# Pauses between all scattered row transfers, and routing one iteration earlier, in a fused attention and mixture-of-experts kernel

## The chip, the cores and the metric

The kernel runs on one NeuronCore of one Trainium2 chip. Its time is the device time of one execution in microseconds (us). The engines are TensorE (PE in the rows), VectorE (DVE), ScalarE (ACT), GpSimd (POOL) and SyncE (SP). SP and ACT also start DMA transfers; the rows name their queues SPq and ACTq.

## The reference, cut to what matters

16 batches of 100 rows of 256 features. Each batch attends over its own context with 16 heads; the result is added to the rows; each row is then normalised, 8 of 32 experts are chosen for it, and their weighted outputs and the output of two shared experts are added.

```python
x = x + xattn(layernorm(x), ctx)            # softmax over causal scores, 16 heads
h = layernorm(x)
scores = sigmoid(h @ gate_w.T)
sc = scores + gate_bias                      # 8 groups of 4 experts; the best 4 groups stay
tki = top_k(masked(sc), 8)[1]                # 8 experts for each row
tkw = 2.5 * scores[tki] / sum(scores[tki])
routed = sum over the 8 experts of tkw * (silu(h @ w_gate) * (h @ w_up)) @ w_down
shared = silu(h @ sh_gate.T) * (h @ sh_up.T) @ sh_down.T
out = x + routed + shared
```

## The kernel before, in words

The program is written out by hand, one stream of instructions for each engine, with semaphores between them. It has four stages.

**Projections** (to about 47 us): keys, values and queries of all 16 batches.

**Attention**, a loop `for i in range(NB)` on each engine, one batch in each iteration. DVE's iteration is `maximum(i)` (L592), `differences(i)` (L601), `residual(i - 2)` (L610 to L618), `shift(i - 2)` (L622) and `outputs_scaled(i - 1)` (L627, L629). ACT takes the exponentials (L428), copies the turned probabilities (L434), finishes the second norm (L439) and takes the tanh of the router's logits (L451). PE computes scores (L872, L877), turns the probabilities (L898), multiplies them with the values (`values`, L924 and L931, which raises `pv_psum`), projects (L941), turns the normed rows (L951) and computes the logits (L884). POOL has one instruction in the chain of the second norm, the power in `row_numbers(B)` (L359), for which DVE's `shift(B)` waits (`rstd2_ready`).

**Routing and scattering**, woven into the attention. Batches are routed in pairs p = 0 to 7. `route(p)` (L646 to L673) chooses the experts on DVE; `positions(p)` (L910 to L913), inside `values` on PE, counts the rows ahead of each row; `positions_read(p)` (L681) and `destinations(p)` (L687 to L693) on DVE turn this into eight row numbers for each row, and raise `dest_ready`. POOL then issues for each batch eight indirect DMAs (`rows_to_experts`, L364), each of which writes the 100 rows of the batch (1,156 bytes each) to places in the DRAM tensor `slots`, where the rows of an expert lie together. For the first 10 batches a memset of a scratch tile `pause` (L370) stands behind each of these DMAs. POOL runs `row_numbers(B)` and `rows_to_experts(B - 5)` in turn, and the last five batches behind the loop.

**Behind the attention**: `shared_gate_up`, `shared_gate` and so on work out part of the shared experts on PE, ACT and DVE; the counts (`count_psum`, L741) and the table of 132 tiles (L747 to L752) follow from the last pair's destinations. 32 DMAs `slots<-pad` fill the end of each expert's rows, 16 issued by SP (L292) once `pad_ready` is raised, and 16 by ACT (L493), which stand behind ACT's fourth shared tanh (L475). SP then waits for all scattered rows, for all pads and for the table, and starts the loads of the tiles (L304). **The tiles**: 132 tiles of 128 rows go through their experts, and POOL adds each result into DRAM with one indirect DMA (L389). At the end three sums are loaded, added and written out.

DVE executes in program order, so all behind a `wait_ge` in its stream waits too; the same holds for each other engine.

Of the kernel before, what the change touches and what calls it, by code (L numbers as in the profile page):

```python
# [18 lines left out]
NB = 16  # L19
# [14 lines left out]
TOPK = 8  # L34
# [27 lines left out]
def block_kernel(nc, x, ctx_t, w_attn, w_gate_t, col_bias, row_bias, gate_bias, w_exp, consts, out_t):  # L62
# [3 lines left out]
    with ExitStack() as top:  # L66
# [88 lines left out]
        pause = tmp("pause", [S, 176])  # L155
# [167 lines left out]
        def _(pool):  # L323
# [37 lines left out]
            def rows_to_experts(B):  # L361
                pool.wait_ge(dest_ready, B // 2 + 1)
                for r in range(TOPK):
                    pool.indirect_dma_start(slots[:], bass.IndirectOffsetOnAxis(ap=dest[:, B % XR, r:r + 1], axis=0),  # L364
                                            xr[:, B % XR, :], None).then_inc(rows_out[B % XR], 16)
                    if B < 10:

                        if B or r:
                            pool.wait_ge(paused, TOPK * B + r)
                        pool.memset(pause[:], 0.0).then_inc(paused, 1)  # L370

            pool.wait_ge(xt_lo_ready, NG)
            pool.wait_ge(v_psum, 2 * NG)
            pool.wait_ge(q_psum, KC * NG)
            for B in range(NB):
                row_numbers(B)
                if B >= 5:
                    rows_to_experts(B - 5)
            for B in range(NB - 5, NB):
                rows_to_experts(B)  # L380

            pool.wait_ge(zero_out, 16 * (2 * NSUM - 1))
# [152 lines left out]
        def _(v):  # L535
# [69 lines left out]
            def residual(B):  # L605
                v.wait_ge(xb_ready, B // BG + 1)
                v.wait_ge(proj_psum, B + 1)
                if B >= 2:
                    v.wait_ge(ht_ready, B - 1)
                v.tensor_tensor(x_all[:, B, :], ps[0:S, 7, 0:D], x_all[:, B, :], ALU.add).then_inc(x1_ready, 1)  # L610
                v.wait_ge(x1_ready, B + 1)
                v.bn_stats(st2[:], x_all[:, B, :]).then_inc(st2_done, 1)
                v.wait_ge(st2_done, B + 1)
                if B >= 4:
                    v.wait_ge(h1_ready, B - 3)
                v.bn_aggr(mv2[:, B % 4, :], st2[:]).then_inc(mv2_done, 1)
                v.wait_ge(mv2_done, B + 1)
                v.tensor_scalar(ve2[:, B % 4:B % 4 + 1], mv2[:, B % 4, 1:2], EPS, None, ALU.add).then_inc(var2_ready, 1)  # L618

            def shift(B):  # L620
                v.wait_ge(rstd2_ready, B + 1)
                v.scalar_tensor_tensor(nmr2[:, B % 4:B % 4 + 1], mv2[:, B % 4, 0:1], -1.0, rstd2[:, B % 4:B % 4 + 1], ALU.mult,  # L622
                                       ALU.mult).then_inc(shift_ready, 1)
# [71 lines left out]
            for i in range(NB):  # L695
                maximum(i)
                differences(i)
                if i >= 2:
                    residual(i - 2)
                if i >= 6 and i % 2 == 0:  # L700
                    route(i // 2 - 3)
                if i >= 2:
                    shift(i - 2)
                if i >= 1:
                    v.wait_ge(pv_psum, i)
                    if i >= 7 and i % 2 == 1:
                        positions_read((i - 7) // 2)
                    outputs_scaled(i - 1)
                if i >= 7 and i % 2 == 1:
                    destinations((i - 7) // 2)  # L710

            def shared_gate(n):
                s = n % 2
# [7 lines left out]
                v.tensor_copy(y_sh[:, :, group_cols(c)], ps[:, 2:2 + KC, 0:TG]).then_inc(sy_ready, 1)  # L721

            residual(14)
            outputs_scaled(15)
            shift(14)
            route(5)
            residual(15)
            shift(15)
            shared_gate(0)
            positions_read(5)  # L730
            destinations(5)
            route(6)
            shared_gate(1)
            positions_read(6)
# [81 lines left out]
        def _(t):  # L816
# [98 lines left out]
            def values(B):  # L915

                t.wait_ge(pt_ready, RG * (B + 1))
                if B:
                    t.wait_ge(ot_ready, B)
                for m in range(KC):  # L920
                    for p in range(2):
                        for r in range(RG):
                            h = 8 * m + 2 * r + p
                            t.matmul(ps[32 * r:32 * r + 32, 6, m * S:(m + 1) * S], v_g[B // BG][:, B % BG, 32 * h:32 * h + 32],  # L924
                                     pt[:, r, (2 * m + p) * S:(2 * m + p + 1) * S], start=(p == 0), stop=(p == 1),
                                     skip_group_check=True)
                if B >= 6 and B % 2 == 0:
                    positions(B // 2 - 3).then_inc(pos_psum, 1)
                for p in range(2):
                    for r in range(RG):  # L930
                        last = t.matmul(ps[32 * r:32 * r + 32, 6, KC * S:2 * KC * S], ones_pad[:, p, :],  # L931
                                        pt[:, r, :].rearrange("k (m p q) -> k m p q", m=KC, p=2)[:, :, p, :],
                                        start=(p == 0), stop=(p == 1), skip_group_check=True)
                last.then_inc(pv_psum, 1)
# [70 lines left out]
            shared_gate_up(0)  # L1005
            t.wait_ge(tanh_ready, 13)
            logits(13, 4, TG)
            t.wait_ge(ot_ready, NB)
            positions(5).then_inc(pos_psum, 1)
            turn_rows(14)  # L1010
            shared_gate_up(1)
            logits(14, 7, D + KC * S)
# [165 lines left out]
```

## Time and profile before

| | |
|---|---|
| median of 3 runs | 616.83 us (616.48 to 617.9) |
| the profiled execution, its own time | 620.36 us |
| its span, first to last instruction | 618.4 us |
| its mean granted TensorE clock | 0.857 |
| first scattered transfer on POOL | 117.02 us |
| start of the last scattered transfer | 314.25 us |
| start of the first tile load | 333.45 us |
| start of the first and of the last add | 344.10 and 587.92 us |

All stretches are in us from the start of the span of the one profiled execution. A wait written in brackets at the end of a row is the idle time of that engine just before the row, with the engine and line that ended it; "remote" and "another core or an unknown queue" there mean that the profile found no event that ended it at that moment, and "issue" that the engine waited for nothing that the profile shows.

### The profile page before, as it was taken

The numbers are of one execution on the slowest core, as the hardware profiler recorded it, in microseconds if no ns is written. First come the engines' busy times: TensorE is split into PE (matmuls) and PEld (weight loads), VectorE is DVE, ScalarE is ACT, GpSimd is POOL, SyncE is SP. The second block draws the span as 40 slices with busy tenths as digits, with TensorE's granted clock in tenths as the row PEclk, the third lists the DMA queues.
The fourth block names the chain that finished last, engine by engine and source line by source line (L and its number), as shares of the span: only waits on it lengthen the run. The fifth ranks groups of instructions, "written<-read, shape, count | busy, mean of one in ns | idle before, by whom it ended". The sixth has DMA issues, their size and how long they took to land.

```text
span 618.4 us, 11702 instructions
## 1 busy us (share of the span) xinstructions
PE 463.4 (75%) x3088; PEld 349.2 (56%) x3089; DVE 344.1 (56%) x1022; ACT 208.9 (34%) x610; POOL 391.7 (63%) x404
## 2 busy tenths in 40 slices
PE   2997986986788474632033999999899999999964
PEld 2895664754455352310012877787787787777633
DVE  5974789777576834621011555555555555555347
ACT  3443465323234320100000554444444444444300
POOL 7560000487877878677730688888888888888810
PEclk9996899579778757666555999999999999999995
DMA  7239130172236227234467577788788778884065
GB/s 210 79 133 351 48 128 29 30 231 87 76 81 223 79 64 271 76 90 119 121 206 180 102 140 140 137 146 141 139 144 142 139 139 143 138 142 95 1 227 198
DMA packets 64792, 82.94 MB, mean 134 GB/s; under 512 B 14272, under 2 KB 53824, under 8 KB 64756
## 3 DMA queue, kind: packets, MB, share of 16 engines
q1 hardware_dynamic: 35252, 52.14, 27.4%
q0 software_dynamic: 27200, 27.98, 26.1%
q10 hardware_dynamic: 2304, 2.37, 1.4%
q8 instruction: 19, 0.31, 0.2%
q14 instruction: 17, 0.14, 0.1%
HBM read 42.67 MB, written 43.93 MB: 140 GB/s over the span
## 4 chain that ended last, share of the span: by engine, by line
PE 23%; issue 21%; POOL 17%; DMA 12%; DVE 12%; another core or an unknown queue 9%; ACTq 2%; ACT 2%; POOLq 1%; SPq 0%; DVEq 0%
POOL slots L364 9%; DMA sums<-ysb,tin 9%; PE ps L1059 7%; POOL sums L389 4%; PE ps L1073 3%; DVE rden L627 2%; PE ps L823 2%; POOL pause L370 2%; PE ps L1050 2%; ACTq L493 2%; DMA fin<-sums 2%; PE ps L988 1%; DVE prob L601 1%; PE ps L941 1%
## 5 line engine op out<-in xcount | busy, mean ns | idle before, releaser
L389 POOL DMA_INDIRECT sums<-ysb,tin x132 | 204.9, 1552 | 69.3 <-ACT ysb L512 33.0
L364 POOL DMA_INDIRECT slots<-xr,dest x128 | 127.8, 998 | 46.8 <-issue 28.7
L1059 PE MATMUL ps<-w_all,hts 128*128 x528 | 137.6, 383 | 8.2 <-issue 5.1
L1059 PEld LDWEIGHTS ps<-w_all,hts 128*128 128x128 f32 x528 | 99.7, 191 | 25.8 <-issue 12.6
L760 DVE COPY hts<-ps 128x256 f32<-128x256 f32 x132 | 56.0, 425 | 80.9 <-PE ps L1050 61.9
L512 ACT ACTIVATE ysb<-ps 128x256 f32<-128x256 f32 x132 | 50.6, 383 | 101.8 <-DMA sums<-ysb,tin 96.0
L1073 PE MATMUL ps<-w_all,ats 128*128 x264 | 83.4, 398 | 0.2 <-ACT ats L504 0.2
L1050 PE MATMUL ps<-cst,tin 128*128 128x128 f32 x264 | 51.6, 278 | 11.6 <-DMA tin<-slots 9.8
L769 DVE SCALAR_TENSOR_TENSOR act_t<-opened_t,tin,ps 128x128 f32<-128x128 f32 x132 | 45.9, 348 | 20.9 <-DVE opened_t L764 12.8
L498 ACT ACTIVATE opened_t<-ps 128x128 f32<-128x128 f32 x132 | 36.3, 275 | 53.7 <-PE ps L1059 44.8
L1050 PEld LDWEIGHTS ps<-cst,tin 128*128 128x128 f32 x264 | 36.6, 142 | 29.1 <-issue 16.7
L898 PE MATMUL ps<-cst,prob 100*100 100x100 f32 x256 | 38.3, 296 | 17.4 <-ACT prob L428 15.3
L359 POOL TENSOR_TENSOR rstd<-ve,cst 100x1 f32<-100x1 f32 x16 | 9.1, 570 | 62.2 <-DVE ve L618 62.2
L764 DVE SCALAR_TENSOR_TENSOR opened_t<-opened_t,ps 128x128 f32<-128x128 f32 x132 | 37.1, 281 | 18.8 <-issue 9.6
L898 PEld LDWEIGHTS ps<-cst,prob 100*100 100x100 f32 x256 | 28.4, 154 | 28.2 <-ACT prob L428 21.1
L941 PE MATMUL ps<-wo,ot 128*100 128x256 f32 x64 | 24.7, 525 | 22.7 <-DVE ot L629 22.7
L1073 PEld LDWEIGHTS ps<-w_all,ats 128*128 128x128 f32 x264 | 39.6, 189 | 3.5 <-issue 0.6
L504 ACT ACTIVATE ats<-ps 128x128 f32<-128x128 f32 x132 | 37.0, 280 | 10.0 <-PE ps L1067 6.8
L998 PE MATMUL ps<-sh_act,w_sh 128*128 128x400 f32 x32 | 15.2, 606 | 33.5 <-issue 28.7
L1067 PE MATMUL ps<-cst,act_t 128*128 128x128 f32 x132 | 37.4, 283 | 3.3 <-DVE act_t L769 2.3
L434 ACT ACTIVATE pt<-ps 100x400 f32<-100x400 f32 x64 | 31.2, 501 | 22.6 <-PE ps L898 18.1
L428 ACT ACTIVATE prob<-prob 100x400 f32<-100x400 f32 x64 | 33.1, 535 | 13.6 <-DVE prob L601 11.7
(156 smaller groups left out, 687.2 us busy)
## 6 DMA issues: line engine op xcount, KB each, us to landing
tin<-slots SPq DMA_DIRECT2D x132, 144.5 KB
w_all<-w_exp SPq DMA_DIRECT2D x3, 2304.0 KB
fin<-sums SPq DMA_DIRECT2D x12, 400.0 KB
sums<-pad SPq DMA_DIRECT2D x2, 1664.0 KB, 8.3
w_all<-w_exp SPq DMA_DIRECT2D x1, 2688.0 KB
slots<-pad SPq DMA_DIRECT2D x17, 144.5 KB, 2.3
slots<-pad ACTq DMA_DIRECT2D x16, 144.5 KB
sums<-ysb,tin POOLq DMA_INDIRECT x132
```

Source lines behind the costliest of these rows:

```text
L364: pool.indirect_dma_start(slots[:], bass.IndirectOffsetOnAxis(ap=dest[:, B % XR, r:r + 1], axis=0), xr[:, B % XR, :], None).then_inc(rows_ ...
L389: pool.indirect_dma_start(sums[j % NSUM][:], bass.IndirectOffsetOnAxis(ap=tin[:, j % RING, ID:ID + 1].bitcast(U32), axis=0), ysb[:, j % YR ...
L504: a.activation(ats[:, s % 2, :], ps[:, 4 + s % 2, 0:P], ACT.Copy).then_inc(at_ready, 1)
L512: a.activation(ysb[:, s % YR, :], ps[:, 6 + s % 2, 0:D], ACT.Copy).then_inc(yt_ready, 1)
L760: v.tensor_copy(hts[:, s % 2], ps[:, s % 2, 0:KC * P].rearrange("p (k t) -> p k t", k=KC)).then_inc(lt_ready, 1)
L764: v.scalar_tensor_tensor(opened_t[:, 2 + s % 2, :], opened_t[:, s % 2, :], 1.0, ps[:, 2 + s % 2, 0:FI], ALU.add, ALU.mult).then_inc(opened, 1)
L769: v.scalar_tensor_tensor(act_t[:, s % 2, :], opened_t[:, 2 + s % 2, :], tin[:, s, bass.ds(e + WT, 1)], ps[:, 2 + s % 2, FI:2 * FI], ALU.mu ...
L898: last = t.transpose(ps[0:S, 4 + r % 2, j * S:(j + 1) * S], prob[:, B % 2, r, j * S:(j + 1) * S], ident[0:S, 0:S])
L1050: last = t.transpose(ps[:, s % 2, k * P:(k + 1) * P], tin[:, s, k * P:(k + 1) * P], ident)
L1059: last = t.matmul(ps[:, 2 + s % 2, 0:2 * FI].rearrange("p (t n) -> p t n", t=2), hts[:, s % 2, k, :], w[:, k], start=(k == 0), stop=(k == ...
L1067: t.transpose(ps[:, 4 + s % 2, 0:P], act_t[:, s % 2, :], ident).then_inc(at_psum, 1)
L1073: t.matmul(ps[:, 6 + s % 2, 0:D], ats[:, s % 2, :], w_all[:, bass.ds(e, 1), 2 * D:].rearrange("p o n -> p (o n)"), start=True, stop=True). ...
```

## The change

Three things are edited. First, the memset of `pause` follows every scattered DMA, where it followed those of batches 0 to 9. Second, on DVE `route(p)` moves from iteration 2p + 6 to iteration 2p + 5, and `destinations(p)` from 2p + 7 to 2p + 6; both, and `outputs_scaled`, now stand ahead of `shift` in the iteration. PE's `positions(p)` moves from `values(2p + 6)` to `values(2p + 5)`. Third, POOL scatters batch B - 4 behind `row_numbers(B)`, where it scattered batch B - 5.

```diff
                     pool.indirect_dma_start(slots[:], bass.IndirectOffsetOnAxis(ap=dest[:, B % XR, r:r + 1], axis=0),
                                             xr[:, B % XR, :], None).then_inc(rows_out[B % XR], 16)
-                    if B < 10:
-
-                        if B or r:
-                            pool.wait_ge(paused, TOPK * B + r)
-                        pool.memset(pause[:], 0.0).then_inc(paused, 1)
+
+                    if B or r:
+                        pool.wait_ge(paused, TOPK * B + r)
+                    pool.memset(pause[:], 0.0).then_inc(paused, 1)
...
             for B in range(NB):
                 row_numbers(B)
-                if B >= 5:
-                    rows_to_experts(B - 5)
-            for B in range(NB - 5, NB):
+                if B >= 4:
+                    rows_to_experts(B - 4)
+            for B in range(NB - 4, NB):
                 rows_to_experts(B)
...
                 if i >= 2:
                     residual(i - 2)
+                if i >= 1:
+                    v.wait_ge(pv_psum, i)
+                    if i >= 6 and i % 2 == 0:
+                        positions_read(i // 2 - 3)
+                    outputs_scaled(i - 1)
                 if i >= 6 and i % 2 == 0:
-                    route(i // 2 - 3)
+                    destinations(i // 2 - 3)
+                if i >= 5 and i % 2 == 1:
+                    route((i - 5) // 2)
                 if i >= 2:
                     shift(i - 2)
-                if i >= 1:
-                    v.wait_ge(pv_psum, i)
-                    if i >= 7 and i % 2 == 1:
-                        positions_read((i - 7) // 2)
-                    outputs_scaled(i - 1)
-                if i >= 7 and i % 2 == 1:
-                    destinations((i - 7) // 2)
...
             residual(14)
+            v.wait_ge(pv_psum, NB)
+            positions_read(5)
             outputs_scaled(15)
+            destinations(5)
             shift(14)
-            route(5)
             residual(15)
             shift(15)
             shared_gate(0)
-            positions_read(5)
-            destinations(5)
             route(6)
...
-                if B >= 6 and B % 2 == 0:
-                    positions(B // 2 - 3).then_inc(pos_psum, 1)
+                if B >= 5 and B % 2 == 1:
+                    positions((B - 5) // 2).then_inc(pos_psum, 1)
...
             t.wait_ge(tanh_ready, 13)
             logits(13, 4, TG)
-            t.wait_ge(ot_ready, NB)
-            positions(5).then_inc(pos_psum, 1)
             turn_rows(14)
```

On DVE, the end of the iteration that gives pair 0 its destinations; before, this is iteration 7 (`ve` is the last row of `residual(5)`, `nmr` is the shift):

```order
L618 TENSOR_SCALAR ve<-mv 100x1 [waits mv2_done]
L622 SCALAR_TENSOR_TENSOR nmr<-mv,rstd 100x1 [waits rstd2_ready]
L681 TENSOR_TENSOR rt<-ps,ebase 100x64 [waits pos_psum,tables_ready,pv_psum]
L627 RECIPROCAL rden<-ps 128x200 [waits pv_psum]
L629 TENSOR_TENSOR ot<-ps,rden 128x200 [waits rden_ready]
L687 SCALAR_TENSOR_TENSOR rt<-rt 100x64 [waits pos_ready]
L688 MAX best_d<-rt 100x8 [waits routing_step]
L688 MAX best_d<-rt 100x8
L690 TENSOR_SCALAR dest<-best_d 100x16 [waits weights_ready,routing_step]
```

The same place in the change, which is now iteration 6 (`ve` is the last row of `residual(4)`; the lines are one lower here):

```order
L617 TENSOR_SCALAR ve<-mv 100x1 [waits mv2_done]
L680 TENSOR_TENSOR rt<-ps,ebase 100x64 [waits pos_psum,tables_ready,pv_psum]
L626 RECIPROCAL rden<-ps 128x200 [waits pv_psum]
L628 TENSOR_TENSOR ot<-ps,rden 128x200 [waits rden_ready]
L686 SCALAR_TENSOR_TENSOR rt<-rt 100x64 [waits pos_ready]
L687 MAX best_d<-rt 100x8 [waits routing_step]
L687 MAX best_d<-rt 100x8
L689 TENSOR_SCALAR dest<-best_d 100x16 [waits weights_ready,routing_step]
L691 TENSOR_TENSOR run_mid<-mask_m 100x32
L692 TENSOR_TENSOR run<-run,run_mid 100x32 [waits routing_step]
L621 SCALAR_TENSOR_TENSOR nmr<-mv,rstd 100x1 [waits rstd2_ready]
```

The shift, which waits for POOL, has moved from ahead of the destinations to behind them, and the wait for `pv_psum` from behind the shift to ahead of it.

On POOL, the end of the scattering before, from the last `row_numbers` on:

```order
L357 IOTA xr 100x1 [waits rows_out7]
L359 TENSOR_TENSOR rstd<-ve,cst 100x1 [waits var2_ready]
L364 DMA slots<-xr,dest 55424x289 [waits dest_ready]
L364 DMA slots<-xr,dest 55424x289 x7
L364 DMA slots<-xr,dest 55424x289 [waits dest_ready]
L364 DMA slots<-xr,dest 55424x289 x7
```

In the change the rows there are these, and they go on in pairs of a DMA and a memset to the end:

```order
L357 IOTA xr 100x1 [waits rows_out7]
L359 TENSOR_TENSOR rstd<-ve,cst 100x1 [waits var2_ready]
L364 DMA slots<-xr,dest 55424x289 [waits dest_ready]
L369 MEMSET pause 100x176 [waits paused]
L364 DMA slots<-xr,dest 55424x289
L369 MEMSET pause 100x176 [waits paused]
L364 DMA slots<-xr,dest 55424x289
L369 MEMSET pause 100x176 [waits paused]
```

Before, the first DMA behind the last `row_numbers` is that of batch 10; in the change it is that of batch 11. The 48 DMAs of batches 10 to 15 each have a memset behind them now.

## Rows read from the trace of the kernel before

**Rows 1.** The page's head.
```profile
span 618.4 us, 11702 instructions
```

**Rows 2.** Chain that ended last, its end ahead of the tiles: start us, us, what.
```profile
325.85 6.44 DMA slots<-pad
```

**Rows 3.** DMA issues of SP and ACT in order of time, merged: start, us.
```profile
286.21 38.58 SPq L292 DMA_DIRECT2D slots<-pad  x16
333.45 6.07 SPq L304 DMA_DIRECT2D tin<-slots  x12
308.26 18.16 ACTq L493 DMA_DIRECT2D slots<-pad  x16
```

**Rows 4.** POOL in order of time: last scatter's start, adds; [idle before].
```profile
254.82 0.98 POOL L364 DMA_INDIRECT slots<-xr,dest  x1 [0.31 <-issue]
...
314.25 0.99 POOL L364 DMA_INDIRECT slots<-xr,dest  x1 [0.30 <-issue]
344.10 1.62 POOL L389 DMA_INDIRECT sums<-ysb,tin  x1 [28.86 <-ACT ysb L512]
...
587.92 1.55 POOL L389 DMA_INDIRECT sums<-ysb,tin  x1 [0.30 <-issue]
```

**Rows 5.** PE, ACT and DVE behind the attention, in order of time.
```profile
275.43 5.70 PE L988 MATMUL ps<-h_all,w_sh 128*128 128x400 f32 x8
306.88 0.50 ACT L475 ACTIVATE sh_act<-ps 128x400 f32<-128x400 f32 x1 [41.59 <-remote]
313.18 0.28 DVE L747 TENSOR_TENSOR begun<-jota,ps 32x132 f32<-32x132 f32 x1 [26.98 <-remote]
```

**Rows 6.** 253 to 285 us: busy PE, PEld, DVE, ACT, POOL; clock, DMA share, GB/s.
```profile
253.00:285.00 32.00, 17.46 (x55) 9.05 (x54) 12.53 (x79) 1.63 (x5) 24.22 (x25) 0.71 0.30 85
```

**Rows 7.** POOL grouped, 117 to 253 us: busy us, mean ns | idle before us.
```profile
L364 POOL DMA_INDIRECT slots<-xr,dest x80 | 80.3, 1004 | 29.9 <-DVE dest L690 15.5 <-issue 14.4
L370 POOL MEMSET pause<- 100x176 f32 x80 | 20.9, 261 | 0.1
```

**Rows 8.** POOL in order of time, batches 2 and 3, each one's first.
```profile
144.57 1.04 POOL L364 DMA_INDIRECT slots<-xr,dest  x1 [3.04 <-DVE dest L690]
...
156.84 1.04 POOL L364 DMA_INDIRECT slots<-xr,dest  x1 [0.22 <-issue]
```

**Rows 9.** DVE, PE and ACT in iteration 11, under transfers with memsets.
```profile
160.25 2.01 DVE L601 TENSOR_TENSOR prob<-ps,nm 100x400 f32<-100x400 f32 x4
164.75 0.62 PE L898 MATMUL ps<-cst,prob 100*100 100x100 f32 x5 [0.28 <-issue]
168.56 0.20 ACT L451 ACTIVATE th<-ps 100x32 f32<-100x32 f32 x1 [6.37 <-remote]
174.65 1.24 PE L931 MATMUL ps<-pt,ones_pad 100*32 100x200 f32 x16
```

**Rows 10.** DVE in order of time, iterations 5 and 6, and pair 0.
```profile
94.85 0.16 DVE L622 SCALAR_TENSOR_TENSOR nmr<-mv,rstd 100x1 f32<-100x1 f32 x1 [0.67 <-POOL rstd L359]
96.65 1.88 DVE L592 TENSOR_REDUCE nm<-ps 100x8 f32<-100x800 f32 x2
101.58 0.20 DVE L646 TENSOR_SCALAR rt<-th 100x64 f32<-100x64 f32 x1
106.27 0.15 DVE L622 SCALAR_TENSOR_TENSOR nmr<-mv,rstd 100x1 f32<-100x1 f32 x1
115.92 0.22 DVE L687 SCALAR_TENSOR_TENSOR rt<-rt 100x64 f32<-100x64 f32 x1
116.49 0.18 DVE L690 TENSOR_SCALAR dest<-best_d 100x16 uint32<-100x16 f32 x1
```

**Rows 11.** DVE: the last shift, and the destinations of pairs 6 and 7.
```profile
250.96 0.16 DVE L622 SCALAR_TENSOR_TENSOR nmr<-mv,rstd 100x1 f32<-100x1 f32 x1 [5.99 <-POOL rstd L359]
261.36 0.18 DVE L690 TENSOR_SCALAR dest<-best_d 100x16 uint32<-100x16 f32 x1
274.80 0.35 DVE L690 TENSOR_SCALAR dest<-best_d 100x16 uint32<-100x16 f32 x1
```

## The prediction, made before the changed kernel had run

> **What bounds the kernel now.** The whole span is 618.4 us [rows 1]. I read it from the end backwards. POOL's adds are the pace of the tiles: the first starts at 344.10, the last at 587.92 [rows 4], 131 steps of 1.861 us with 0.3 us of idle time between them. They begin 10.65 us behind the first tile load (333.45 [rows 3]). So the stage of the tiles moves as a block with the first tile load, and neither its length nor what follows is touched by the change. The question is what sets 333.45.
>
> The chain of what ended last, read there, shows a DMA `slots<-pad` that was issued at 325.85 and landed 6.44 us later, at 332.3 [rows 2]. The timeline of the issues shows the pads late on both queues: SP needs 38.58 us for its 16, from 286.21 to 324.8, and ACT starts its 16 only at 308.26 [rows 3]. POOL's last scatter starts at 314.25 [rows 4], so it is over 18 us ahead of the tile load and not itself the last wait.
>
> Why are the pads late? ACT's stand behind its fourth shared tanh. That one waits for matmuls of PE which end at 281.13 (275.43 + 5.70), and runs at 306.88, 25.8 us later; the profile calls the wait "remote", which is to say that it saw no event there. DVE's `begun` waits for the same engine's signal, and comes at 313.18 after 26.98 us [rows 5]. In that stretch the DMA engines are busy to 0.30 only, at 85 GB/s [rows 6], so it is no lack of bandwidth. What is special there is POOL: 48 scatters without a memset between them, one each 1.292 us (46 steps from 254.82 to 314.25 [rows 4]). Earlier, with memsets, the same kind of lateness exists and is small: PE's transposes are done at 165.37 and ACT's next instruction starts at 168.56, 3.2 us later [rows 9]. I read this as a signal of PE that is held back while POOL issues transfers back to back, 3 us with memsets and some 26 without. That is the reading on which the forecast rests.
>
> **The change, step by step.** *The memsets.* With one, a transfer costs 1.004 + 0.261 us and 0.18 us of idle time (14.4 us over 80), 1.445 us together [rows 7]; without, 1.292. 48 transfers get one: 48 x 0.153 = +7.3 us on POOL.
>
> *Routing earlier.* Pair 0's destinations now come at 116.49 [rows 10]. In the new order iteration 5 loses the wait of 0.67 us for POOL and gains the routing, 106.27 - 101.58 = 4.69 us, which hides that wait. Iteration 6 then starts at 96.65 + 4.69 - 0.67 = 100.7. From there, 4.93 us to the end of the residual part (101.58 - 96.65), 0.15 for reading the positions (half a vector instruction of this size, an estimate from the 0.2 us rows), 1.73 for `outputs_scaled` (96.65 - 94.92), 0.75 for the destinations (116.67 - 115.92) [rows 10]: 108.3. POOL starts 0.4 us later, at 108.7, some 8 us earlier than now.
>
> *The waits in the loop.* A batch with its `row_numbers` takes POOL 156.84 - 144.57 = 12.27 us [rows 8]. Now POOL waits once in each pair for destinations, 15.5 us in five waits [rows 7], because they stand behind the shift, which stands behind POOL's power, which stands behind the batch before. In the new order they stand ahead of the shift, so POOL finds them ready unless DVE itself is late. If POOL never waits, batches 0 to 10 take 11 x 12.27 = 135.0 and batches 11 to 15, with no `row_numbers` between them, 5 x 8 x 1.445 = 57.8: the last transfer is over at 108.7 + 192.8 = 301.5.
>
> *The new wait in front of the shift.* `pv_psum` of PE is now awaited ahead of the shift, with the routing or the destinations, the shift, the next maximum and, through `nmr`, ACT's second norm and PE's `turn_rows` queued behind it. From the end of the differences of iteration 11 (162.26) to the end of PE's sums (175.89) are 13.6 us [rows 9], with a lateness of 3.2 already in them; the signal itself may be another 0 to 3.2 late. From there DVE needs 1.73 + 4.69 + 3.9 (maximum and differences: 4.93 less some 1.1 for the residual part, an estimate) to the differences two iterations on: 13.6 + 10.3 = 23.9 to 27.1 us for two batches, where POOL needs 24.5. So POOL loses 0 to 2.6 us in each of 5.5 pairs, 0 to 14 us. I take 0.7 for each, 4 us, nearer to the lower end, since not every iteration shows the lateness.
>
> *Behind the loop.* The last shift, now at 250.96 [rows 11], comes when batch 10 is scattered: 108.7 + 135.0 - 0.6 + 4 = 247. Pair 6's destinations follow 10.4 us later now (261.36 [rows 11]); 1 us of pair 5's work is no longer there, and two or three of PE's signals on this path will be some 2 us late each, as POOL no longer stands still here: 261. POOL is ready for them at 247 + 0.6 + 11.6 = 259, so it waits 2 to 4 us; I take 3. Its last transfer ends at 301.5 + 4 + 3 = 308.5 and lands by about 310. Pair 7's destinations come 13.4 us after pair 6's now; I keep 10 to 13 of them, 272.
>
> *The pads.* SP starts 11.4 us after pair 7's destinations now (286.21 - 274.80). If the signal of the counts is 3 us late and not nine, it starts at 278. Its 16 take 38.6 us at the worst, by the row, and 16 x 0.5 = 8 us at the best, by the spacing of the tile loads (6.07 for 12 [rows 3]); nearest is the row of the pads themselves, eased by the memsets, and I take 32: 310. ACT's start at about 290, for PE's matmuls end near 281 and the signal is 5 to 9 us late; 18 us later they are issued. Landing takes 2 to 6 us: all pads are down at 314, and the first tile load starts at 315.5.
>
> **The sum.** 333.45 - 315.5 = 18 us less, against the profiled execution's own 620.36 us; the median of the runs is 3.5 us below that, and I take the same difference there, 616.83 - 18 = 599, rounded to 600. The bounds: at best nothing waits and the pads keep up, so POOL's end at 301.5 and a landing of 2 us decide, tile load at 304.5, 29 us less, 588. At worst for this mechanism POOL waits 14 + 4 us (end 319.5, tile load at 323), 10 us less, 606.5. So 588 to 607 for the likeliest case itself.
>
> **A rule against this reading.** The profile has ACT and DVE waiting for PE, with transfers in the background, and I make the transfers the cause [rows 5, 6]. The Trainium skill, "SBUF — State Buffer", section "Who interferes with whom", says that a DMA never contends with a compute engine, and that only the port pair which VectorE and GpSimd share makes one op hold up another. By it the memsets would buy nothing and cost their 7.3 us, which is the first rival below, at 612. No run here has tried it; the trace's 3.2 us with memsets against 25.8 us without speaks for the other side, but the two stand in different parts of the program.
>
> **Rivals.** *The lateness is not due to missing memsets.* Then signals behind the attention stay as late, and only the earlier end of the loop counts: pair 7's destinations come about 4 to 5 us earlier (250.96 to 247), ACT's pads with them, and POOL's longer scattering, over at 308.5, stays ahead of them. 616.83 - 5 = 612. For it: SP's pads last until 324.8 [rows 3], 10 us after POOL has issued its last transfer [rows 4]. Against it: the size of the lateness. Chance 0.15.
>
> *The full gain.* Nothing in the loop is late and SP's pads take under 25 us: 588 to 592, 0.12.
>
> *Slower: PE's late signal holds DVE ahead of the shift.* Both iterations of a pair pay the 3.2 us, so that POOL waits 2.8 us a pair more than nothing, 15.4 in 5.5 pairs, and another 7 for pair 6: POOL ends at 301.5 + 22 = 324, 9 us later than its 315.2 now. If the rest still trails it by 18.2 us (333.45 - 315.24), the time is 616.83 + 9 = 626. It decides from 13.7 us of waits on, with the trail unchanged. Against it: with memsets up to the end, the pads ought not to trail so far. Chance 0.08.
>
> *No effect:* the gains and the memsets' cost cancel, as a trail of 18 us and 13 us of waits would have it: 617, chance 0.03.
>
> **How the numbers follow.** The likeliest case, 588 to 607 around 600, has 0.62. With the full gain and the first rival there is 0.89. The range from 589 to 613 holds most of the likeliest, the first rival and part of the full gain, and leaves out less than 2 in 10. 0.2% of 616.83 is 1.2 us, about what a measurement of this kernel can tell from no change. Faster by more than that: 0.89; within: 0.03; slower: 0.08.
>
> **What would show it.** Right: the first scatter near 108.7; POOL's waits for `dest` under 8 us in all; no "remote" wait over 10 us on ACT or DVE behind the attention; SP's pads from about 278 and ACT's from about 290; the first tile load between 304 and 323; adds still 1.86 us apart. Wrong: ACT's fourth shared tanh still 20 us behind PE, with a memset behind each transfer (the lateness has another cause); or POOL waiting over 13 us for destinations while DVE waits for `pv_psum`.

## The result, and the profile after

The changed kernel takes 595.5 us (median of 4 runs, 591.59 to 598.66) against 617.37 in the runs of the kernel before beside them: ratio 0.963, 95% interval 0.955 to 0.971. It is faster by 22 us, where 17 were forecast.

The profiled execution was the fastest of its four: 591.59 us, its span 589.5.

I read it as the one before, from the end of the chain backwards. The chain of waits around the first tile load (start, us, what):

```profile
298.66 0.99 POOL slots L364
300.10 2.82 DMA slots<-xr,dest
303.19 0.77 SPq L237
304.14 0.37 SPq L304
304.70 2.39 DMA tin<-slots
```

In the place of the late pad of [rows 2] stands POOL's own last scatter. The first tile load is at 304.14 where it was at 333.45 [rows 3], and it follows the start of the last scatter (300.10) by 4.04 us where it followed by 19.20 (333.45 - 314.25 [rows 3, 4]). I call this distance the trail. Some of the expectations below put it at 5.5 us for the change: they count from 298.66, the last scatter but one.

The timeline of the issues on SP and then on ACT, with the tanh that ACT's pads stand behind:

```profile
261.74 13.86 SPq L292 DMA_DIRECT2D slots<-pad  x16
304.14 24.65 SPq L304 DMA_DIRECT2D tin<-slots  x18
...
264.38 0.50 ACT L474 ACTIVATE sh_act<-ps 128x400 f32<-128x400 f32 x1 [8.39 <-issue]
267.17 17.25 ACTq L492 DMA_DIRECT2D slots<-pad  x16
```

SP issues its 16 pads in 13.86 us instead of 38.58 and is done at 275.6. ACT's end at 284.4, and the tanh shows no remote wait where it had 41.59 us [rows 3, 5]: PE's matmuls for it end at 264.34, and it starts at 264.38. All pads are down long before the last scatter.

DVE there, for comparison with [rows 5] and [rows 11]:

```profile
243.50 0.16 DVE L621 SCALAR_TENSOR_TENSOR nmr<-mv,rstd 100x1 f32<-100x1 f32 x1 [9.84 <-POOL rstd L359]
253.54 0.20 DVE L689 TENSOR_SCALAR dest<-best_d 100x16 uint32<-100x16 f32 x1
259.49 0.17 DVE L689 TENSOR_SCALAR dest<-best_d 100x16 uint32<-100x16 f32 x1
264.72 0.28 DVE L746 TENSOR_TENSOR begun<-jota,ps 32x132 f32<-32x132 f32 x1 [2.95 <-issue]
```

`begun` waits 2.95 us and not 26.98. The stretch of [rows 6], same columns: the DMA engines are busy to 0.82 of it, where they were to 0.30, and still neither the tanh nor `begun` is late. So it was not their load that made them late before.

```profile
253.00:285.00 32.00, 12.81 (x44) 6.17 (x42) 11.43 (x54) 1.01 (x2) 27.83 (x45) 0.81 0.82 201
```

POOL in order of time, the first and the last of the five scatters that waited for destinations (the three between waited 0.40, 2.66 and 1.10 us):

```profile
102.63 1.22 POOL L364 DMA_INDIRECT slots<-xr,dest  x1 [2.27 <-DVE dest L689]
...
206.87 1.04 POOL L364 DMA_INDIRECT slots<-xr,dest  x1 [2.59 <-DVE dest L689]
```

and POOL grouped from 95 to 320 us, the counterpart of [rows 7] with all 128 scatters:

```profile
L364 POOL DMA_INDIRECT slots<-xr,dest x128 | 128.1, 1001 | 32.7 <-issue 23.7 <-DVE dest L689 9.0
L369 POOL MEMSET pause<- 100x176 f32 x128 | 33.6, 262 | 0.2
```

Behind its first scatter POOL waits 6.7 us for destinations (9.0 less the 2.27 ahead of the first). Before, it waited 14.7 there: the 15.5 of [rows 7] hold the 3.33 us ahead of the first scatter and leave out 2.54 at 253.47, for pair 5. Pairs 5 to 7 now cost no wait. Last, what is still late inside the attention (waits grouped, 100 to 320 us: engine, line, what for, us in total, times, longest):

```profile
ACT th L450 <- remote: 47.7, 9, 7.1
...
DVE rden L626 <- remote: 15.9, 5, 5.1
...
DVE nmr L621 <- POOL rstd L359: 14.0, 3, 9.8
```

In these profiles the tile load comes 29.3 us earlier. That splits into the start of the scattering, 14.4 (117.02 to 102.63), its length from first to last scatter, -0.3 (197.2 to 197.5), and the trail, 15.2. The length hides three things that cancel: 8.0 us less of waiting (14.7 to 6.7), 7.3 us of new memsets, and 0.7 us for one more `row_numbers` between the first and the last scatter (12.27 less 8 x 1.445), since POOL starts one batch earlier. Both profiled executions lie off their medians, the one before 3.5 us above and this one 3.9 us below, so some 7 of the 29.3 us are the choice of executions.

### The profile page after: what moved, and what is told of

It reads as the page before. It is cut to its first block, busy times and chain, and to the rows that moved or that the text cites. A ratio compares the mean times of both kernels' runs of the same rounds, so it can differ in the third digit from the quotient of the medians.

```text
span 589.5 us, 11751 instructions
## 1 busy us (share of the span) xinstructions
PE 465.6 (79%) x3088; PEld 352.6 (60%) x3089; DVE 343.2 (58%) x1022; ACT 207.2 (35%) x610; POOL 405.0 (69%) x452
## 4 chain that ended last, share of the span: by engine, by line
PE 28%; POOL 18%; DVE 17%; issue 16%; DMA 11%; another core or an unknown queue 5%; ACT 3%; POOLq 0%; SPq 0%; DVEq 0%; ACTq 0%
POOL slots L364 11%; PE ps L1056 10%; DMA sums<-ysb,tin 8%; PE ps L1070 5%; PE ps L822 4%; POOL sums L388 3%; PE ps L1047 3%; DVE prob L600 3%; POOL pause L369 3%; DVE rden L626 2%; DVE nm L591 2%; PE ps L1064 2%; DMA fin<-sums 2%; PE ps L897 1%
## 5 line engine op out<-in xcount | busy, mean ns | idle before, releaser
L897 PE MATMUL ps<-cst,prob 100*100 100x100 f32 x256 | 41.2, 308 | 20.4 <-ACT prob L427 18.8
L763 DVE SCALAR_TENSOR_TENSOR opened_t<-opened_t,ps 128x128 f32<-128x128 f32 x132 | 37.2, 282 | 20.9 <-issue 13.7
L897 PEld LDWEIGHTS ps<-cst,prob 100*100 100x100 f32 x256 | 29.8, 161 | 31.8 <-ACT prob L427 27.2
L987 PE MATMUL ps<-h_all,w_sh 128*128 128x400 f32 x64 | 28.6, 603 | 10.9 <-issue 10.9
L591 DVE TENSOR_REDUCE nm<-ps 100x8 f32<-100x800 f32 x32 | 30.1, 983 | 8.0 <-PE ps L876 8.0
```

The costliest lines, as they stand in the source:

```text
L591: v.tensor_reduce(nm[:, 8 * i:8 * i + 8].rearrange("p (r n) -> p r n", r=2), ps[0:S, 2 * i:2 * i + 2, 0:TG].rearrange("p r (n k) -> p r n ...
L763: v.scalar_tensor_tensor(opened_t[:, 2 + s % 2, :], opened_t[:, s % 2, :], 1.0, ps[:, 2 + s % 2, 0:FI], ALU.add, ALU.mult).then_inc(opened, 1)
L897: last = t.transpose(ps[0:S, 4 + r % 2, j * S:(j + 1) * S], prob[:, B % 2, r, j * S:(j + 1) * S], ident[0:S, 0:S])
```

## The experiments

A time is the median of the runs of that kernel, the ratio is against the kernel before on the same chip (medians of 619.4 to 621.8 us there). The experiments ran on three chips, so differences between them are best taken from the ratios. An "unpaced" scatter is one with no memset behind it. "Memsets" are the pauses behind POOL's scatters. "First", "last" and "tile load" are the starts of the first scatter, the last scatter and the first tile load in its profile.

**The change once more**, beside the experiments.

> The changed kernel once more, as the comparison for the three beside it. Expected at 592 to 599 us, with the first scattered transfer near 103 us, the start of the last one near 299 and the first tile load some 5.5 us behind it (298.66 and 304.14 in its first profile). If the first profile was a lucky one, the last transfer starts up to 5 us later, since the four executions so far spread from 591.6 to 598.7.

Measured: 593.81 us (592.44 to 600.33), ratio 0.959 (0.954 to 0.965), as expected. First 102.60, last 302.02, tile load 306.06. It is the yardstick for what follows.

**The memsets alone, in the old order.**

```
-                    if B < 10:
-
-                        if B or r:
-                            pool.wait_ge(paused, TOPK * B + r)
-                        pool.memset(pause[:], 0.0).then_inc(paused, 1)
+                    if B or r:
+                        pool.wait_ge(paused, TOPK * B + r)
+                    pool.memset(pause[:], 0.0).then_inc(paused, 1)
```

> The kernel before, with a memset behind all 128 transfers and nothing else changed. My theory: back-to-back transfers hold PE's signals back, and memsets release them. Then POOL's last transfer starts 48 x 0.153 = 7.3 us later than before, at 321.6; ACT's fourth shared tanh and DVE's begun run within 8 us of PE's matmuls; all pads are down ahead of POOL's end; and the first tile load is 5.5 us behind the last transfer's start, at 327: 6.4 us earlier than before, 610 us. Rival (the lateness has another cause, and the new order removed it): the tanh stays some 20 us late, the tile load stays at 333 or moves with POOL's extra 7.3 us, 617 to 624 us.

Measured: 610.68 us (609.92 to 611.89), ratio 0.985 (0.980 to 0.989), as expected. The issues and the tanh:

```profile
266.50 10.81 SPq L292 DMA_DIRECT2D slots<-pad  x16
322.47 27.18 SPq L304 DMA_DIRECT2D tin<-slots  x19
...
270.53 0.50 ACT L473 ACTIVATE sh_act<-ps 128x400 f32<-128x400 f32 x1 [10.14 <-issue]
273.17 14.48 ACTq L491 DMA_DIRECT2D slots<-pad  x16
```

The last scatter starts at 318.42, so the trail falls from 19.2 to 4.05 us with nothing changed but the memsets. That POOL's unpaced scatters made the pads late is shown, and so is the price: the last scatter is 4.2 us later than before although the first is 3.0 earlier, at 114.01. Those 3.0 us are there before any scatter (see "First scatter" below) and are not the memsets' doing.

**The new order alone**: memsets behind batches 0 to 9 as before.

```
-                    if B or r:
+                    if B < 10:
+                        if B or r:
...
```

> The changed kernel with memsets behind the transfers of batches 0 to 9 only, as before: the new order alone. My theory: the last transfer starts at 298.7 - 7.3 = 291.3, but the signals behind the attention are late by 20 us or more again, ACT's pads start about when POOL ends, and the trail from the last transfer's start to the tile load is again about 19 us: tile load at 310, 602 us. Rival (memsets do nothing for the signals): the trail is 5.5 us, tile load at 297, 588 us, faster than the changed kernel.

Measured: 595.46 us (593.37 to 601.86), ratio 0.961 (0.955 to 0.967), the same as the whole change. Neither expectation fits.

```profile
265.62 37.56 SPq L292 DMA_DIRECT2D slots<-pad  x16
307.95 40.33 SPq L304 DMA_DIRECT2D tin<-slots  x26
...
269.08 0.50 ACT L475 ACTIVATE sh_act<-ps 128x400 f32<-128x400 f32 x1 [11.23 <-issue]
271.05 33.17 ACTq L493 DMA_DIRECT2D slots<-pad  x16
```

The pads crawl as before, 37.56 us on SP and 33.17 on ACT, and the trail is 10 us. But the tanh is on time, with no memsets near it:

```profile
263.76 5.28 PE L988 MATMUL ps<-h_all,w_sh 128*128 128x400 f32 x8
```

PE ends at 269.04 and the tanh starts at 269.08. It isn't that it came early in POOL's unpaced stretch: that began at 234.19, 35 us ahead of it, while before it began at 253.47, 28 us ahead of the end of PE's matmuls (281.13), and the tanh came 25.8 us late. Two later signals are late even so, by 5.5 us (PE's L1035 ends at 272.86, DVE's `tab` starts at 278.36) and by 4.9 (L998 at 283.26, `y_sh` at 288.16). Why the new order alone shrinks the lateness behind the attention from some 26 us to 5.5 at most is not shown. ACT's pads thus start 37 us earlier than before (308.26 [rows 3]), and the crawl ends at 304.2, some 6 us behind the last scatter (298.00). In time the crawl costs no more here than the memsets do.

**Memsets behind batches 0 to 12**, the last three batches without.

```
-                    if B or r:
+                    if B < 13:
+                        if B or r:
...
```

> The changed kernel with memsets for batches 0 to 12 and none for 13 to 15. In the profile of the changed kernel batch 13 begins at 266.9, when DVE has read the counts (260.1) and begun (264.7), and only the pads are under way. My theory: nothing that the tiles need is waited for any more, so POOL saves 24 x 0.153 = 3.7 us and the tile load follows: 592 us against 595.5. Rival: the pads of SP and ACT, issued until 284.4 then, slow down without memsets to the pace of before (2.4 us for each of SP's) and land behind POOL's end at 296: no gain, or some us slower.

Measured: 591.04 us (587.86 to 592.83), ratio 0.952 (0.947 to 0.957), as expected. Pads: SP 12.38 us from 262.79, ACT 18.00 from 269.84. Tile load 301.14, trail 4.2. The rival was that the pads crawl again. They don't, although the last memset starts at 266.73 and all of ACT's pads are issued beside unpaced scatters:

```profile
267.19 0.99 POOL L364 DMA_INDIRECT slots<-xr,dest  x1 [0.19 <-issue]
268.49 0.99 POOL L364 DMA_INDIRECT slots<-xr,dest  x1 [0.30 <-issue]
...
269.84 18.00 ACTq L493 DMA_DIRECT2D slots<-pad  x16
```

ACT needs 18.00 us with the unpaced stretch begun 3 us earlier, and 33.17 in the new order alone, with it begun 37 us earlier. So the pace of the moment doesn't set the crawl by itself; something in the stretch ahead of it counts too. What it is, and how long a stretch is harmless, no run shows.

**Memsets only behind batches 10 to 15**: the loop of the attention runs under unpaced scatters.

```
-                    if B or r:
-                        pool.wait_ge(paused, TOPK * B + r)
+                    if B >= 10:
+                        if B > 10 or r:
+                            pool.wait_ge(paused, TOPK * (B - 10) + r)
...
```

> The changed kernel with memsets behind the transfers of batches 10 to 15 only, none for 0 to 9. So far the new order without the late memsets (595.5 us) and with them (593.8) were the same within their spread, so it is open what memsets do in the loop, where ACT's tanh of the logits is late in every iteration with them. My theory (back-to-back transfers hold PE's signals back): DVE gets pv_psum later, POOL waits for destinations well over the 9 us of now, and the 80 x 0.153 = 12.2 us saved on POOL are lost again; 594 us or more. Rival (in the loop memsets only cost POOL time): the last transfer starts 12 us earlier, at 288, the first tile load at 292, 582 us.

Measured: 628.6 us (625.42 to 634.6), ratio 1.012 (1.005 to 1.020): the direction of the theory, and far beyond its 594. Its waits, in the view and the window shown above of the change:

```profile
ACT th L451 <- remote: 69.7, 5, 17.3
POOL rstd L359 <- DVE ve L618: 53.5, 6, 11.7
DVE rden L627 <- remote: 46.4, 5, 12.5
```

And one such wait in order of time, with PE's work that it needs (`L931` gives `rden`; `th` needs `L884` and, by the program, the first four transposes, `L898`):

```profile
111.05 0.54 PE L931 MATMUL ps<-pt,ones_pad 100*32 100x200 f32 x3 [0.18 <-issue]
111.52 0.73 PE L884 MATMUL ps<-wg,h_all 128*100 128x32 f32 x4
112.52 0.50 PE L898 MATMUL ps<-cst,prob 100*100 100x100 f32 x4 [0.27 <-issue]
...
119.81 1.41 DVE L627 RECIPROCAL rden<-ps 128x200 f32<-128x200 f32 x1 [7.66 <-remote]
...
121.88 0.20 ACT L451 ACTIVATE th<-ps 100x32 f32<-100x32 f32 x1 [11.28 <-remote]
```

PE is done with the sums at 111.59 and with the transposes at 113.02; DVE starts 8.2 and ACT 8.9 us later, and the profile names nothing else that they wait for. The 80 memsets of the loop are worth some 33 us (1.012 less 0.959, of 620) although they take POOL 80 x 0.153 = 12 us.

**The same with short rows**, to see whether the moved bytes do it: scatters, pads and tile loads carry 132 bytes of a row and not 1156. Left out are the features, which are the experts' input (zeros are used).

```
-                                            xr[:, B % XR, :], None).then_inc(rows_out[B % XR], 16)
+                                            xr[:, B % XR, ID:], None).then_inc(rows_out[B % XR], 16)
...
```

> The kernel with memsets in the tail only (628.6 us, no memsets for batches 0 to 9), but each row that is scattered, padded and loaded has 132 bytes, not 1,156: number, weight factors, no features, which are zero from a memset of tin behind POOL's last transfer. So this leaves the experts' inputs out, and only the stretch up to the tiles is to be compared. If it is the bytes of the transfers that hold PE's signals back, the loop runs as with memsets: POOL waits under 12 us for DVE, the last transfer starts near 290 or earlier. If it is POOL's issuing (descriptors and their signals, the same number as before), the lateness stays: remote waits of 17 us, the last transfer starts near 335 as in that kernel. I lean to the second.

Measured: 632.36 us, one run. From 107 to 232 us the memsets-in-the-tail kernel and this one (two traces, same columns as [rows 6]):

```profile
107.00:232.00 125.00, 86.91 (x723) 54.13 (x719) 67.45 (x229) 33.31 (x80) 68.76 (x79) 0.67 0.34 105
```

```profile
107.00:232.00 125.00, 89.15 (x657) 56.40 (x657) 64.38 (x224) 31.19 (x75) 65.58 (x76) 0.59 0.17 52
```

Half the DMA share and half the bytes a second, and the lateness is the same or larger:

```profile
ACT th L454 <- remote: 75.6, 5, 17.3
```

So it doesn't go with what the transfers carry. Their number and pace were the same in both.

**How long a pause?** The pause tile has 176 columns; 88, 132 and 352 were tried, in the new order, behind every scatter.

```
-        pause = tmp("pause", [S, 176])
+        pause = tmp("pause", [S, 88])
```

> The changed kernel with a pause tile of 88 columns, not 176. If the memset's time is proportional to its columns beyond a fixed part of about 0.15 us (the iota of one column takes 0.15, the memset of 176 takes 0.26), it takes 0.21 and a transfer 1.39 us: 128 x 0.055 = 7 us less on POOL. My theory: half the pause still lets the signals through, since what counts is that the next transfer waits for the memset at all: last transfer at 293, 587 us. Rival: the length of the gap counts; remote waits of over 8 us come back behind the attention and the pads take over 25 us, 592 us or more.

> The changed kernel with a pause tile of 132 columns, between 176 (593.8 us) and 88 (614.0). The memset takes (0.189 + 0.263) / 2 = 0.226 us, a transfer every 1.41 us where it is 1.45 and 1.37. If what counts is a rate that must not be passed, something between 1.37 and 1.45 is passed or it is not: either POOL gains 128 x 0.037 = 4.7 us and the time is 589, or the late signals are back in the loop and the time lies near 605 or above. If the lateness grows evenly with the rate, the time is half way, 604. I lean to the last.

> The changed kernel with a pause tile of 352 columns: the memset takes 0.189 + 264 x 0.00084 = 0.41 us, a transfer every 1.59 us. My theory: the lateness of PE's signals in the loop shrinks further; remote waits of ACT's tanh fall from 59 us in ten to under 20, POOL no longer waits for destinations except at its first batch; POOL itself takes 128 x 0.147 = 18.8 us more and saves 8 us of waits: 605 us. Rival: the lateness in the loop does not depend on the pace once it is slow enough; remote waits stay near 50 us, 612 us.

Measured, with the pace worked out as a transfer (1.0 us), its memset and 0.18 us of idle time (the waits for `dest` hold 2.27 us ahead of the first scatter in each row):

| columns | memset ns | pace us | time us | ratio (95%) | `th` remote, longest | POOL's waits for `dest` | SP's pads |
|---|---|---|---|---|---|---|---|
| 88 | 189 | 1.37 | 613.96 | 0.988 (0.981 to 0.996) | 9.5 | 20.5 | 34.26 |
| 132 | 225 | 1.41 | 594.22 | 0.962 (0.956 to 0.968) | 7.5 | 16.6 | 23.08 |
| 176 (again) | 262 | 1.445 | 593.81 | 0.959 (0.954 to 0.965) | 7.4 | 10.7 | 15.05 |
| 352 | 409 | 1.59 | 605.95 | 0.979 (0.974 to 0.985) | none | 2.3 | 14.92 |

That any memset is enough is refuted: with 88 columns the lateness is back, in the loop and behind it. The expectations for 132 leaned to 604 us and were wrong; those for 352 held. Whether the pause has to be a memset was not tried.

```profile
282.70 34.26 SPq L292 DMA_DIRECT2D slots<-pad  x16
...
289.48 0.50 ACT L474 ACTIVATE sh_act<-ps 128x400 f32<-128x400 f32 x1 [14.30 <-remote]
291.27 29.59 ACTq L492 DMA_DIRECT2D slots<-pad  x16
```

With 132 the shorter memsets save 128 x 0.037 = 4.7 us of POOL and 5.9 more go into waits for destinations. With 352 all remote waits but one of 1.2 us are gone, but the longer memsets take POOL 128 x 0.147 = 18.8 us and give back 8.4 in waits for destinations, 10.4 us together where 12 were measured. Between 132 and 176 the time is flat.

**The shift ahead of outputs and destinations again**, with the earlier routing and all memsets kept.

```
+                if i >= 5 and i % 2 == 1:
+                    route((i - 5) // 2)
+                if i >= 2:
+                    shift(i - 2)
                 if i >= 1:
...
                     destinations(i // 2 - 3)
-                if i >= 5 and i % 2 == 1:
-                    route((i - 5) // 2)
-                if i >= 2:
-                    shift(i - 2)
...
```

Routing keeps its iteration and stands ahead of the shift and of `outputs_scaled`, as in the kernel before.

> The changed kernel, with DVE's shift put back ahead of outputs_scaled and of the destinations; routing stays in odd iterations and POOL at B - 4. My theory: each pair's destinations stand again behind POOL's power of the batch before, so POOL waits some 3.05 us per pair as before, 15 us in five waits where the changed kernel has 6.7: the last transfer starts 8 us later, 602 us; and the early iterations are 6.7 + 0.75 us long again, the first transfer at 105 to 106. Rival: it is the earlier routing alone that counts; no more waits than now, 595 us.

Measured: 606.2 us (604.18 to 608.25), ratio 0.975 (0.968 to 0.983). First 109.67, last 316.84, tile load 320.89.

```profile
POOL slots L364 <- DVE dest L689: 20.0, 6, 3.4
```

POOL waits in each of six pairs again, 3.3 us each, as the theory has it. The first scatter is 7 us later, 3.8 of which are there before any scatter and are not the order (66.90 for 63.13 us, see "First scatter" below). By the ratios this place in the order is worth 10 us, by the medians 12.

**POOL one batch further behind** (five, not four).

```
-                if B >= 4:
-                    rows_to_experts(B - 4)
-            for B in range(NB - 4, NB):
+                if B >= 5:
+                    rows_to_experts(B - 5)
+            for B in range(NB - 5, NB):
```

> The changed kernel, but POOL scatters batch B - 5 behind row_numbers(B), as before. POOL's first transfer must then wait for the variance of batch 5, one DVE iteration later: start at about 108.4 us, not 102.6. In return the destinations of a pair are ready an iteration ahead, so that POOL never waits in the loop (7 us less), and one batch fewer stands in the loop. 108.4 + 10 x 12.27 + 11.6 + 57.8 = 300.5: the last transfer starts at 299.4 against 300.1, the time is that of the changed kernel within 2 us. Rival: the distance of four is what brings the gain; then the time is 6 us longer, the later start uncompensated, 600 us.

Measured: 593.62 us (590.98 to 597.71), ratio 0.955 (0.947 to 0.962), no change, as expected. First 112.86 (4.5 us later than expected, 4.1 of them there before any scatter), last 303.64: POOL starts 10 us later, waits for destinations nowhere, and is done within 2 us of the change repeated. The 10.7 us of waits in that one are thus the price of starting early and no loss.

**Both spared**: POOL five behind, memsets behind batches 0 to 11.

```
-                    if B or r:
+                    if B < 12:
+                        if B or r:
...
-                if B >= 4:
-                    rows_to_experts(B - 4)
+                if B >= 5:
+                    rows_to_experts(B - 5)
...
```

> The changed kernel with POOL at batch B - 5, as in the run of that name, and memsets only behind the transfers of batches 0 to 11. There POOL never waited for destinations, the counts were read at about 252 and all pads were issued by 275, while batch 12 begins near 259. My theory: back-to-back transfers do harm only while others still wait for signals. From 259 on only some pads are left, so the last transfer starts 32 x 0.153 = 4.9 us earlier and the tile load follows it by 4: 589 us. Rival: the pads still under way crawl (2.4 us each on SP, 2.1 on ACT) and land behind POOL's end: 593 us or more.

Measured: 589.57 us (587.62 to 591.79), ratio 0.953 (0.949 to 0.957), as expected. Pads: SP 13.15 us from 250.47, ACT 17.65 from 255.92, beside scatters without memsets from 255.12 on; tile load 299.62. With the memsets to batch 12 (0.952) it is the best version; the two can't be told apart.

## Why the prediction was right, and where its steps were off

Sign and size held: 595.5 us lies in the range and in the likeliest case's own. The mechanism held for the kernel before, and not for the changed one, where the new order alone gives the whole gain. And in part the number came out by luck: the first tile load was forecast 18 us earlier and came 29 us earlier in the profiles; some 7 of these 29 are the choice of executions. Step by step:

- **The trail is due to missing memsets: right.** It was read from two parts of the program that are not alike; memsets alone in the old order took it from 19.2 to 4.05 us. The first rival (612) falls with that. But they are not the only cure: the order alone took it to 10 us. By the Trainium skill, "SBUF — State Buffer", section "Who interferes with whom", which stood behind the first rival, a DMA never contends with a compute engine. To the letter the runs don't contradict it: fewer bytes don't lessen the lateness. The time goes another way than was drawn from it: ACT and DVE do lose time while transfers are issued, by starting late behind PE.
- **First scatter 108.7: it was 102.63.** Two terms were missing. The step counted POOL's round trip as hidden only in iteration 5; but `outputs_scaled` stands ahead of the shift in every iteration, so that from iteration 2 to 5 the maxima come 6.72 us apart and not 7.48, 3 x 0.76 = 2.3 us. The other 3.6 us are there at the third maximum already. Before:

```profile
66.73 1.89 DVE L592 TENSOR_REDUCE nm<-ps 100x8 f32<-100x800 f32 x2 [2.26 <-PE ps L877]
74.22 1.88 DVE L592 TENSOR_REDUCE nm<-ps 100x8 f32<-100x800 f32 x2
```

The same in the change:

```profile
63.14 1.89 DVE L591 TENSOR_REDUCE nm<-ps 100x8 f32<-100x800 f32 x2 [0.24 <-PE ps L876]
69.87 1.88 DVE L591 TENSOR_REDUCE nm<-ps 100x8 f32<-100x800 f32 x2
```

That part is not the order: the old order with memsets has its third maximum at 63.76, the new order with memsets in the tail at 67.36. It lies ahead of all scatters, and seems to differ from one execution to the next: the five profiles with a late third maximum (65.69 to 67.36) lie 2 to 6 us above the medians of their kernels, those with an early one between 3.9 below and 1.2 above. What causes it is not shown.

- **Memsets, +7.3 us: right** as POOL's time (33.6 us for 128, 262 ns each, against 80 before).
- **POOL's waits, 4 + 3 us: they were 6.7 in the loop and none for pair 6.** Pair 6's destinations came at 253.54, not 261: the last shift came 3.5 us earlier (243.50, not 247), and the signals behind it were on time, where I had put 2 us on each. Pair 7's came at 259.49, not 272. Their distance to pair 6's, 5.95 us for 13.44 before, had held a signal 6.7 us late (PE's L913 ends at 267.30, DVE's L681 starts at 273.96); in the new order alone it is 5.9 too. The slower rival (`pv_psum` ahead of the shift) needed 13.7 us of waits; there were 6.7.
- **Last transfer over at 308.5: it was over at 301.1**, 6 us of it from the earlier start.
- **SP's pads from 278 taking 32 us, ACT's from 290: from 261.74 taking 13.86, and from 267.17.** They start early mostly because pair 7's destinations were 12.5 us earlier than I had them. The duration was mis-sized most. Of two ends, 8 and 38.6 us, I took the one near the row, "eased by the memsets". But that row was itself measured under scatters without memsets. So the path that ends last was wrong: I had the pads there (314), and it is the last scatter. That is the one half of the full-gain rival's condition (pads under 25 us); the other, nothing late in the loop, did not come true (47.7 us of remote waits), and its 588 to 592 were not reached.
- **Tile load 315.5: it was 304.14**, and 306.06 in the second profile. The time is not as far off as that, because the profile before lies above its median and that after below.

Which edit brings the 22 us? They overlap. The memsets alone give 10, the order alone 26, both together 27 (on one chip, against 621.0, where the result itself has 22). In the new order the 48 added memsets buy nothing that can be measured, and those behind the last three batches cost some 3 us, at the edge of what the intervals tell. Of the order, the shift's place is worth 10 to 12. Two kernels with all memsets and the shift in its old place have 0.985 without the earlier routing and 0.975 with it, some 6 us, with intervals that overlap by a little. They differ in POOL's distance too (five and four batches), which changed nothing measurable in the order of the change; routing earlier was not tried by itself. So the prediction was right about what the missing memsets did to the kernel before, and wrong in leaving the new order out of the cure: it expected late signals to stay until memsets took them away, where in the new order without those memsets the signals behind the attention are 5.5 us late at most.

**Open.** How PE's signal is held up is not shown. The profile shows that PE has ended, that the waiting instruction starts later, and no event between. In the loop without memsets the DMA engines are busy to 0.34 only, and with short rows (0.17) the lateness stays. Nor is it shown why the new order alone lessens the lateness, or why pads issued soon after the last memset don't crawl. The delay may build up over a stretch of unpaced transfers; that would fit the pads, but not the tanh of the new order alone, which is on time 35 us into one.

## What to carry to other kernels

Where an engine waits "remote" on a producer that has long ended while POOL issues indirect transfers back to back, look at the pace of those transfers: stretch it a little, try two or three lengths, and stop the pauses once nobody waits for a signal any more. Put an instruction that waits for POOL behind those that POOL itself waits for; that was worth 10 to 12 us here, where the 48 added pauses bought nothing beside it. Before adding a cure, see whether another edit in the same change already brings it. And take a duration that was measured under the disturbance as an upper bound only: here the cure took it from 38.58 us to 13.86, where "eased" had been read as 32.

## What was not expected of the hardware

- **The lateness has an edge.** From 1.37 to 1.41 us for a transfer, 0.04 us, the time falls by 20 us (613.96 to 594.22; 16 by the ratios). From there to 1.445 the remote waits hardly change, and at 1.59 all but one of 1.2 us are gone.
- **Other engines' DMA issues crawl too.** In the new order alone SP's and ACT's pads take 2.1 to 2.4 us each (37.56 and 33.17 for 16), with 1.445 us pace 0.7 to 1.1, and 1.1 also beside unpaced scatters that began only 3 us earlier (memsets behind batches 0 to 12). The chain of the new order alone shows them in pieces of 0.70 us:

```profile
290.92 0.71 ACTq L493
291.62 0.69 issue
292.31 0.71 ACTq L493
```

- **PE itself is broken up.** With no memsets in the loop a group of `L877`, 16 matmuls, comes as 7 and 9 with a gap of issue between them:

```profile
116.23 1.81 PE L877 MATMUL ps<-k,q 32*100 32x200 f32 x7
118.28 2.42 PE L877 MATMUL ps<-k,q 32*100 32x200 f32 x9 [0.24 <-issue]
```

With memsets it happens too. This is part of such a group in the kernel before:

```profile
178.81 0.74 PE L877 MATMUL ps<-k,q 32*100 32x200 f32 x3
179.83 1.31 PE L877 MATMUL ps<-k,q 32*100 32x200 f32 x5 [0.29 <-issue]
```

From 107 to 227 us the waits of PE that are put down to issue add up to 17.9 us with no memsets in the loop, 3.9 in the kernel before, 1.8 in the change, 9.6 with POOL five behind and 1.3 with 352 columns. What they cost is not shown.
